# Norms of a four-layer graph network: statistics, scaling and transposes folded into the linear ahead of them, and linears that wait tile by tile

## The reference

```
xn = layernorm(x)
x = x + gnn(xn, edges) + mix(xn)        # graph part (attention over edges), linear attention
x = x + ffn(layernorm(x))               # soft or top-2 mixture of experts
```

```
L0: heads k and v of the mix are normed per head (64 features) with weights g, b
L1: mix: k, q, v = linears of xn; phi(k) needs k * k; ffn: router(layernorm(x)), top 2 of 8 experts
L2: gnn: two graph attention layers, the second one's linear has 1024 rows
    mix: y = xn;  y = y + attn(ln1(y));  y = y + fc2(gelu(fc1(ln2(y))))     # ln1, ln2 with weights w, b
    ffn: h = layernorm(x); a = ln1(h) -> q, k, v; h = h + attn @ out_w; h = h + mlp(h);
         xm = ln2(h) -> gate, 4 experts, top 2; x = x + h + moe(xm)         # ln1, ln2 with weights g, b
L3: gnn (two layers, 1 head), mix with norm at its end, ffn with 8 experts
```

## Time and profile before

| | |
|---|---|
| median of 3 runs | 3376.29 (3374.47 to 3378.44) |
| profiled execution | 3373.8, of which the span of the trace is 3371.9 |
| mean granted TensorE clock | 0.923 |
| PE busy | 2793.9 (83%) |
| DVE, ACT, POOL busy | 1451.6 (43%), 1006.9 (30%), 738.8 (22%) |
| mean DMA rate | 66 GB/s |

### The profile page before, as it was taken

The page is one execution under the profiler, slowest core; times in us unless marked ns, Lnnn a source line. Parts: engine busy times, 40 slices in busy tenths (PEclk is TensorE's granted clock), DMA queues, the critical chain, the costliest instruction groups (busy, mean ns, idle before and its releaser), DMA issues. The chain is left out here.

```text
span 3371.9 us, 47798 instructions
## 1 busy us (share of the span) xinstructions
PE 2793.9 (83%) x19943; PEld 2524.5 (75%) x19943; DVE 1451.6 (43%) x3349; ACT 1006.9 (30%) x1769; POOL 738.8 (22%) x314
## 2 busy tenths in 40 slices
PE   7788979996768898987859799979887779798587
PEld 7688978994338778976858799968556777596587
DVE  8953256653122224447453532243755541303633
ACT  0123235650003112228431142223532232255121
POOL 2332221100004112240234233331013231012222
PEclk9899989998699999998979899989998889899789
DMA  2022120004982101210111122212001211000011
GB/s 64 1 62 66 59 85 29 24 24 181 413 334 69 34 29 48 68 61 23 38 61 44 51 75 71 72 61 62 1 8 50 66 62 43 23 29 30 20 57 61
DMA packets 158969, 224.21 MB, mean 66 GB/s; under 512 B 16969, under 2 KB 136451, under 8 KB 158754
## 3 DMA queue, kind: packets, MB, share of 16 engines
q1 hardware_dynamic: 158754, 221.15, 19.5%
HBM read 219.20 MB, written 1.92 MB: 66 GB/s over the span
## 5 line engine op out<-in xcount | busy, mean ns | idle before, releaser
L47 PE MATMUL ps<-weights_r,buf_r 128*125 128x256 f32 (+2 forms) x4000 | 541.3, 288 | 46.5 <-DVE buf_r L2613 15.1
L47 PEld LDWEIGHTS ps<-weights_r,buf_r 128*125 128x125 f32 (+1 forms) x4000 | 515.2, 189 | 50.3 <-issue 43.7
L250 POOL TENSOR_TENSOR weights_r<-weights,weights_r 128x1536 fp32r<-128x1536 f32 (+1 forms) x79 | 269.9, 3416 | 1122.1 <-ACT weights_r L243 1122.1
L250 POOL TENSOR_TENSOR weights_r<-weights,head_weights_r 128x1536 fp32r<-128x1536 f32 (+1 forms) x78 | 270.0, 3462 | 1109.7 <-ACT head_weights_r L243 1109.7
L47 PE MATMUL ps<-xT_r,weights_r 128*128 128x376 f32 (+1 forms) x2100 | 347.1, 311 | 0.0
L47 PE MATMUL ps<-head_weights_r,buf_r 128*125 128x256 f32 (+1 forms) x2330 | 324.7, 285 | 0.0
L47 PEld LDWEIGHTS ps<-xT_r,weights_r 128*128 128x128 f32 x2100 | 316.2, 189 | 3.9 <-issue 1.1
L47 PEld LDWEIGHTS ps<-head_weights_r,buf_r 128*125 128x125 f32 x2330 | 300.9, 189 | 0.0
L824 PE MATMUL ps<-ident,buf 125*128 125x125 f32 x645 | 106.1, 334 | 180.7 <-DVE buf L899 99.0
L47 PE MATMUL ps<-weights_r,xT_r 128*125 128x256 f32 x1650 | 232.6, 285 | 27.7 <-DVE buf_r L688 8.7
L824 PEld LDWEIGHTS ps<-ident,buf 125*128 125x128 f32 x645 | 94.1, 178 | 193.2 <-issue 160.9
(11 more groups left out here) (300 smaller groups left out, 4318.3 us busy)
## 6 DMA issues: line engine op xcount, KB each, us to landing
expert_regions<-in_L_ffn_w SPq DMA_DIRECT2D x64, 576.0 KB, 15.1
expert_regions<-in_L_ffn_w SPq DMA_DIRECT2D x48, 768.0 KB, 15.6
weights<-in_L_mix_fc_w SPq DMA_DIRECT2D x24, 768.0 KB, 4.5
weights<-in_L_gnn_W SPq DMA_DIRECT2D x18, 768.0 KB, 4.6
weights<-in_L_ffn_W SPq DMA_DIRECT2D x12, 768.0 KB, 4.7
weights<-in_L_mix_w_mapT SPq DMA_DIRECT2D x9, 768.0 KB, 4.6
weights<-in_L_gnn_W_out SPq DMA_DIRECT2D x9, 768.0 KB, 4.8
weights<-in_L_mix_kqv_wT SPq DMA_DIRECT2D x9, 768.0 KB, 4.6
```

The costliest lines, as they stand in the source:

```text
L47: mm = net.nc.tensor.matmul(ps, net.r(stationary(s, k)), net.r(moving(m, k)), start=(n == 0 and k == 0), stop=(n == 2 and k == kc - 1))
L250: self.nc.gpsimd.tensor_tensor(self.r(load.dst), load.dst, self.r(load.high), ALU.subtract).then_inc(self.low_made, 1)
```

## The change

**LinearNorm.** A new stage joins a linear that adds to a buffer, the norm of that buffer and the transposes. It is used at seven places: the sum of experts ahead of the norm of L1 (two units of 384 columns, one matmul each), the projection of L1's mix ahead of the router's norm, w2 of L1's experts ahead of L2's norm, the projection of L2's mix ahead of ln2, the last quarter of fc2 ahead of the double norm, mlp_w2 ahead of ln2 of the ffn, and exp_w2 ahead of L3's norm. In every unit DVE makes the statistics of the columns just added. In the last unit it does per tile: add, `bn_stats`, `bn_aggr`, the low halves of tile t - 3, reciprocal, scaling. ACT takes per tile the root with eps as its bias and makes the high halves of tile t - 2. PE puts the transposes of tile t - 2 behind the product of tile t. ACT splits weights for the stages behind ahead of the roots, but for the last unit, which it splits after them.

**Norm weights as feature columns** (`columns`). At three of the places the norm has weights. They are no longer rows multiplied before the transpose but columns of 128 numbers per chunk: ACT copies each chunk of 125 columns from PSUM with the weight as scale and the bias as bias, then makes the high half of three chunks from that, and DVE one low half a tile. Six such columns sets are loaded among the constants at the start, as single numbers.

**Double norm** (`first`). At the double norm of L2's ffn both roots are taken per tile in the fused stage; the once normed buffer X itself is made by a new stage `Normalise` on POOL, beside the main line, ahead of the AddRow on X.

**Order.** ln1 of L2's mix moves ahead of the two linears W2T that it does not depend on; its transposes stay behind them, and the first of these linears is evacuated by ACT alone. In L0 the linear for v stands ahead of HeadNorm of k. Several linears wait for the same start (`after=start`) in place of all before them.

**Tile waits** (`tiles`). A Linear or LinearT behind transposes waits in its first unit for the halves of the tile that it reads, in place of the whole stage ahead. Buffers are renamed where the new order needs it.

```diff
+class LinearNorm(Linear):
+    def tensor(self, pe):
+        if self.tiles is None:
+            self.begin(pe)
+        for i in range(NT * len(self.units)):
+            self.product(pe, i, self.bank["product", i])
+            if i - self.last >= 2:
+                self.turn(pe, i - self.last - 2)
+        for t in range(NT - 2, NT):
+            self.turn(pe, t)
...
+    def vector(self, dve):
...
+        for i in range(NT * len(self.units)):
+            self.wait(dve, "pe", "product", i)
+            evacuate(nc, "d", "add", ...)
+            dve.wait_ge(done.sem, done.issued)
+            nc.vector.bn_stats(self.net.moments[:, tile, o:o + 6], self.x[:, tile, i // NT * w:(i // NT + 1) * w])
+            if t < 0:
+                continue
+            dve.wait_ge(done.sem, done.issued)
+            nc.vector.bn_aggr(mv[:, t, :], self.net.moments[:, t, 0:n])
+            if t >= 3:
+                low(t - 3)
+            self.wait(dve, "act", "root", t)
+            nc.vector.reciprocal(col(self.rstd, t), col(self.rstd, t))
+            dve.wait_ge(done.sem, done.issued)
...
+            nc.vector.tensor_scalar(self.out[:, t], self.x[:, t], mv[:, t, 0:1], col(rstd, t), ALU.subtract, ALU.mult)
+        for t in range(NT - 3, NT):
+            low(t)
...
+    def scalar(self, act):
...
+        for load in self.weights[:-1]:
+            self.net.split_high(load.unit + 2, load.segment)
+        for t in range(NT):
+            self.wait(act, "dve", "mean", t)
+            nc.scalar.activation(self.rstd[:, t:t + 1], self.net.mv[:, t, 1:2], ACT.Sqrt, bias=self.net.eps[self.first or self.eps][:TP, :])
...
+            if t >= 2:
+                high(t - 2)
+        for t in range(NT - 2, NT):
+            high(t)
+        for load in self.weights[-1:]:
+            self.net.split_high(load.unit + 2, load.segment)
...
+class Normalise(Stage):
+    side = True
+    def gpsimd(self, pool):
+        self.begin(pool)
+        for t in range(NT):
+            self.nc.gpsimd.tensor_scalar(self.out[:, t], self.x[:, t], self.net.mv[:, t, 0:1], self.rstd[:, t:t + 1], ALU.subtract, ALU.mult)
...
 # Linear, first unit (LinearT: tiles[min(t1, NT - 1)] for each of its two products)
+        if self.tiles is not None and i < NT:
+            pe.wait_ge(*self.tiles[t])
...
 # start of network
+    for name in ("L2_mix_ln2_w", "L2_mix_ln2_b", "L2_ffn_ln1_g", "L2_ffn_ln1_b", "L2_ffn_ln2_g", "L2_ffn_ln2_b"):
+        norm_cols[name] = net.cols[:, net.ncol:net.ncol + KC]
+        net.ncol += KC
+        net.const(norm_cols[name], ins[name].rearrange("o (c p) -> p (o c)", p=128))
...
 # L0
     linear(net, XT, w, tok(G[1]), cols=(D, 2 * D), evac="a")
-    head_norm = HeadNorm(net, heads(G[1]), ..., 1e-5)
-    linear(net, XT, w, tok(G[3]), cols=(2 * D, 3 * D), evac="a")
     made = now()
-    linear_T(net, XT, ins["L0_gnn_W_ah"], feat(G[5]), bias=col["b_ah_c"], kind="relu", evac="a")
+    linear(net, XT, w, tok(G[3]), cols=(2 * D, 3 * D), evac="a", after=start)
+    head_norm = HeadNorm(net, heads(G[1]), ..., 1e-5, made)
+    made = now()
+    linear_T(net, XT, ins["L0_gnn_W_ah"], feat(G[5]), bias=col["b_ah_c"], kind="relu", evac="a", after=start)
...
 # L2, gnn and mix
-    ToFeatures(net, tok(G[4]), outT[0], "relu")
-    ToFeatures(net, outB, outT[1], "relu")
-    linear(net, outT[0], ins["L2_gnn_W2T"], tok(G[4]), rows=(0, D))
-    linear(net, outT[1], ins["L2_gnn_W2T"], tok(G[4]), "add", add=tok(G[4]), rows=(D, 1024))
-    XT = pair(net.XT, G[1])
-    norm_T(net, tok(G[5]), tok(G[0]), XT, 1e-8, net.row(ins["L2_mix_ln1_w"]), net.row(ins["L2_mix_ln1_b"]))
+    turned = ToFeatures(net, tok(G[4]), outT[0], "relu")
+    turned2 = ToFeatures(net, outB, outT[1], "relu")
+    norm = LayerNorm(net, tok(G[5]), tok(G[1]), 1e-8, net.row(ins["L2_mix_ln1_w"]), net.row(ins["L2_mix_ln1_b"]))
+    linear(net, outT[0], ins["L2_gnn_W2T"], tok(G[4]), rows=(0, D), evac="a", after=turned2.after + turned2.ends(), tiles=turned.made)
+    linear(net, outT[1], ins["L2_gnn_W2T"], tok(G[4]), "add", add=tok(G[4]), rows=(D, 1024), tiles=turned2.made)
+    XT = pair(net.XT, G[0])
+    turned = ToFeatures(net, tok(G[1]), XT, evac="a")
...
 # L2, double norm of the ffn
+    normed = linear_norm(net, pair(G[1], G[3]), ins["L2_mix_fc2_w"], R, tok(G[0]), XT, 1e-5, [norm_cols[n] for n in ("L2_ffn_ln1_g", "L2_ffn_ln1_b")], 1e-5,
+                         rows=(3 * D, 4 * D), after=start + made[3].ends() + added.ends())
     X = tok(G[5])
-    LayerNorm(net, R, X, 1e-5, ready=True)
-    norm_T(net, X, tok(G[0]), XT, 1e-5, net.row(ins["L2_ffn_ln1_g"]), net.row(ins["L2_ffn_ln1_b"]))
-    bias_out = AddRow(net, X, net.row(ins["L2_ffn_out_b"]))
+    scaled = Normalise(net, R, X, normed.rstd)
+    bias_out = AddRow(net, X, net.row(ins["L2_ffn_out_b"]), now() + scaled.ends())
```

316 lines of the change are left out of this document (226 added, 90 removed).

## The result

The changed kernel took 3290.35 us (median of 4 runs, 3287.33 to 3292.84) against 3376.07 for the kernel before on the same chip: ratio 0.9745, 95% interval [0.9728, 0.9762], 86 us faster. Forecast were 3284, 92 us faster, with 3252 to 3322 as range. The profiled execution has a span of 3285.2, against 3371.9. The sum was 6 us too good; by the traces the fused stages in it were 15 too good, which other terms, and a stretch in which the clock happened to stay up, partly made up for.

What follows compares the result with a forecast made beforehand. DVE was taken to bound the eight norm windows, with PE nearly full elsewhere. Gains of 39.6 + 15.3 + 13 + 6.4 + 3.8 + 17.8 less 4 for the start made 91.9 us: 3284 for the median, range 3252 to 3322.

Steps and rivals of the forecast that it cites:

- The tails of the fused stages: At seven fused stages, a per-tile count of what remains beyond products; gains sum to 39.6 us.
- they begin when the whole stage ends, 2.2 us behind the first product now: Two AddRows ahead of the third unit's weight split at L2 start that late; with clock, 2.5 us taken off, leaving 8.9.
- Normalise, "4 us of waiting": Double norm: POOL scaling at 2.2 us each delays the third unit's split; PE waits 4 us, 9.2 us gained.
- ln2 of the ffn, 4.3: Fused stage at 2574.45: products are half as long and hide less, so 4.3 us gained.
- Router and L3: Fused stages before the first router and at 2699.62: 5.1 and 6.4 us gained, after 1.5 off each for the clock.
- The moved norm: Norm moved ahead of a linear, window at 1686.50: its DVE work runs beside products, 15.3 us gained.
- HeadNorm and Square: L0's HeadNorm behind the second linear gains 13 us; PE no longer waiting 5.37 at the Square stage gains 6.4.
- Tile waits: Linears behind transposes at seven places outside the norms save the wait at their end: 16.3 and 1.5 of clock, 17.8 us.
- Rival 1: Fused stages give nothing: tile chain 1.1 us longer, or third unit's weights late at most; gain 52, 3324; chance 0.18.
- rival 4: Whole kernel: waits are renamed and the time stays, 3376; needs Rival 1 and a very full DVE; chance 0.03.
- Rival 2: Clock stays up through tails (8.6 us), no HeadNorm wait comes back (13.6); gain 114, 3262; chance 0.12.
- Rival 3: Slower: POOL's split holds off DVE's scaling of each of 35 fused tiles, 103 us, 3387; chance 0.05.

Runs made afterwards that it cites:

- pool_rows_later: Changed kernel with L2's two AddRows moved to the attention summary's end, and at the double norm Normalise and AddRow each behind a LinearT: 3268.91 us, ratio 0.9691.
- norm_columns_late: Changed kernel with the six sets of norm weight columns loaded behind L0's attention, not among the constants: 3287.48 us, ratio 0.9742.
- square_waits_back: Changed kernel with the second LinearT and the linear for v in L1's mix again waiting for all before them, Square included: 3301.07 us, ratio 0.9780.

## Why the prediction was right, and where its steps were not

- **What bounds it** (DVE in the windows of the earlier trace rows, PE elsewhere): right, but for the column form, where ACT became the bound. Tails of 179.9 us, the moved norm's counted, became 60.4 and one norm beside products.
- **The tails of the fused stages**: counted well, in part by a slip. By its own 3.4 us a tile the scaled tiles 3 and 4 are ready at 14.1 and 17.5 and not at 13.7 and 16.7, and the tail would be 6.1; tiles took 2.3 (2.4 counted) and 2.7 (3.4 counted). 5.5, 10 and 15 us between last product and next linear were announced, 4.4, 11.6 and 16.3 came. `bn_stats` of 256 columns took 0.43 (0.40 taken), an ACT column 0.38 (0.29 taken, upper bound 0.49). The root's table load (1.28 in each stage) lay beside products at five of the seven; at the combine it did not, at ln2 of the ffn only in part. L899 left PE's waits at four fused places, and L910 at the three with weights. The combine lost 3.0 (3.7 forecast).
- **"they begin when the whole stage ends, 2.2 us behind the first product now"**: this is the step that failed. AddRow begins 5.7 behind, because ACT makes the last unit's high half after the norm's and POOL makes its low half, 3.5 us, ahead of AddRow. In the kernel before, that split lay in the norm's window, where POOL had nothing to do. The edit was costed, the split that it moves was not. The two AddRows also took 19.3 us where they had taken 18.1, beside DVE's SelfLoops. At L2 2.5 were taken off and 8.2 went.
- **Normalise, "4 us of waiting"**: by its own terms (2.6 + 20 + 3.5 - 21) that is 5.1. The same split was missing (POOL began 7.0 behind the first product, where 2.6 was taken), and POOL's scaling took 2.92 a tile where 2.2 was taken: 5 x 0.72 = 3.6. PE wanted the weights 1.8 later than counted. The wait was 11.4. By the traces the fused stages gave 14.8 us less than forecast: these two steps lost 13.9 (4.6 at L2, 9.3 at the double norm), ln2 of the ffn 4.7 and ln2 of the mix 1.8, while router, L3 and combine gave 5.6 more than forecast. pool_rows_later, which takes both waits away, gives 18.
- **ln2 of the ffn, 4.3**: came to -0.4. The tail was 12.2 us, and the late Add with the splits behind it cost 4 more at TopTwo. No term of the sum had it.
- **Router and L3**, 5.1 and 6.4, gave 7.4 and 9.0. Of the 1.5 taken off each for the clock, 1.3 came behind the router's tail and nothing behind L3's; which place pays it differs from run to run (last section). These two hid part of what the step above lost.
- **The moved norm**, 15.3: at its place 15.9, with the linear ahead of it 12.2, in the timed runs 10, since its rows hold back a load on SP. The prediction looked at what the move does to DVE and ACT, and not at SP's queue: that is the step that this term missed.
- **HeadNorm and Square**: 13 and 6.4 forecast, 16 and 12 timed (the 12 with one of the five small waits), 13.7 and 6.9 by the traces. The wait of 4.6 for the weights behind the rows was 9.0, the second one of 5.1 was down to 0.9: two misses that cancel. The five small stage waits, 3.8, gave 4.8 with their clock.
- **Tile waits**, 17.8: 19, by the traces 20.8. **The start**, 4: 3.3 by the trace, and norm_columns_late names the loads as its cause.
- **The sum** by the traces: 24.8 + 12.2 + 13.7 + 6.9 + 4.8 + 20.8 - 3.3 = 79.9, 4.5 from the clock in the softmax stretch and 2.3 spread over the rest, 86.7. That the total came within 6 us of the forecast is owed to misses of both signs, and is in part luck.
- **Rival 1** fell (29 timed and not 0), rival 4 with it; but its second half, the third unit's weights late, held at L2 and the double norm, and by the prediction's own signs of being wrong (a linear that waits for a split wherever AddRow follows a fused stage) it came near: of the four such places PE waited 7.1 and 11.4 at two, 1.6 at the combine's (0.9 before) and not at all at L3's. **Rival 2** asked for the clock to stay up, which it did at L3's place and not at the router's or the combine's, and for no wait at HeadNorm, which did not hold. **Rival 3** was right in its mechanism and wrong in its size and place. DVE and POOL hold each other off (last section); in the fused stages' chains only four of the 35 scalings, each beside a split, took 1.7 to 2.1 in place of 0.68, and none of the column form's fifteen low halves took longer than 0.94. It costs 4 us at TopTwo, 8 at the coefficients.

## What to carry to other kernels

When a stage gets shorter, list for each engine's queue what used to run in the hidden part of it: here a weight split lay for free in the norm's window, and two row additions behind it were done just in time (0.3 us of wait); fusing the norm put all three between the linear's start and the weights of its third unit. Read the wait that takes the place of the removed one by its engine (here from DVE's scaling to POOL's split) and move that engine's work to where it is idle; that was worth 18 us more. A load for a moved step moves its slot's wait too, and whatever is behind it on the DMA queue.

## What the runs showed of the hardware

DVE and POOL held each other off when both worked on SBUF. The clearest rows in the changed kernel are two instructions of a scaling, 1.0 us each; the second began 0.1 after a POOL split:

```profile
1611.61 1.01 DVE L1105 SCALAR_TENSOR_TENSOR buf<-buf,stats,row 125x768 f32<-125x768 f32 x1
1612.54 4.25 DVE L1109 SCALAR_TENSOR_TENSOR buf<-buf,stats,row 125x768 f32<-125x768 f32 x1
```

```profile
1612.42 3.56 POOL L252 TENSOR_TENSOR weights_r<-weights,head_weights_r 128x1536 fp32r<-128x1536 f32 x1 [15.22 <-ACT head_weights_r L245]
```

It took 3.2 longer, nearly the whole split. The Trainium skill, "SBUF — State Buffer", section "Who interferes with whom", says that a VectorE instruction with two SBUF inputs contends with a GpSimd one that reads, and that whichever issues first holds the shared ports for its whole instruction while the other is blocked. The rows agree, at 1612.54 for one instruction; at the coefficients both engines got slower in a chain (2.54 against 0.95), which fits turns taken one instruction at a time, though no run isolates that. The 335 additions whose first input is in PSUM (L368) took 0.41 to 0.56 each, none longer, splits or not.

The clock was the second surprise. In the changed kernel's trace the two tails that shrank to 4.4 us kept the full 2.4 GHz, and so did the products behind them; behind the router's tail of 4.8 they fell to 1.2 GHz for 2.2 us, and the longer tails of the column form had a mean of 0.50 to 0.67. But it is not the same in each run. In nine of the twelve traces of kernels with these three tails it was L2's place that paid: a mean of 0.70 to 0.78 over the 4 us behind a tail of 4.8 to 4.9. PE came out of a wait of 5.4 us at the lower level, so a wait that went also shortened the products behind it: Square's 5.5 us brought 1.4 more against the kernel before, and 2.2 against square_waits_back.
